# Linear attention by pairs of heads, V projected with tokens on the partitions, C_acc in the memory of X

## The reference

```python
q, k, v = silu(xn @ w_qkv)              # xn: layer norm of x; per head 128 wide
g = sigmoid(xn @ w_gate)
for each block of tokens:               # the kernel takes blocks of 128
    inter = (q * q_decay) @ kv
    intra = ((q @ k.T) * diag_decay) @ v
    kv = block_decay * kv + (k * k_decay).T @ v
    o = inter + intra
x = x + (rms_norm(o over all heads) * rms_weight * g) @ w_out
```

## Time and profile before

| | |
|---|---|
| median of 3 runs | 3095.34 us (3094.22 to 3097.39) |
| the profiled execution | 3093.59 us |
| its span, first to last instruction | 3091.8 us |
| TensorE, VectorE, ScalarE, GpSimd busy | 2803.0, 1804.6, 1466.3, 793.4 us |
| granted TensorE clock, mean of the span | 0.932 |
| DMA | 193.65 MB, mean 63 GB/s |
| L1789, projections of the linear attention | 342.6 + 322.6 + 321.3 us busy in 3 x 1032 matmuls |
| L1813, transposes VT | 77.2 us busy in 516 |
| L1749, ScalarE's copy of VT | 76.4 us busy in 129 |

### The profile page before, as it was taken

One profiled execution on the slowest core, in us unless ns is written; L12 is line 12 of the kernel. 1 busy time (PEld: TensorE's weight loads), 2 busy tenths in 40 slices (PEclk: granted clock), 3 DMA queues, 4 the chain that ended last, 5 costly groups with the idle time before them and its releaser, 6 DMA issues. The chain is left out here.

```text
span 3091.8 us, 51426 instructions
## 1 busy us (share of the span) xinstructions
PE 2803.0 (91%) x17564; PEld 2237.6 (72%) x17564; DVE 1804.6 (58%) x3284; ACT 1466.3 (47%) x2689; POOL 793.4 (26%) x812
## 2 busy tenths in 40 slices
PE   5689999979889999599999999999999999978573
PEld 4534444448668888488888888988888898868452
DVE  5378888826678887555555555555555545556421
ACT  5337777766468877433333333333333333334110
POOL 2412212210052222022222222222222222214675
PEclk9879999999989999699999999999999999975575
DMA  4875655230064543000000000000000000002376
GB/s 145 238 102 75 84 69 74 30 94 3 4 224 186 189 177 136 23 11 0 10 10 10 10 10 3 8 10 10 10 10 10 0 10 10 8 27 88 90 173 123
DMA packets 159113, 193.65 MB, mean 63 GB/s; under 512 B 18257, under 2 KB 135537, under 8 KB 150257
## 3 DMA queue, kind: packets, MB, share of 16 engines
q1 hardware_dynamic: 150464, 177.10, 21.9%
q0 software_dynamic: 8544, 15.22, 2.9%
HBM read 149.89 MB, written 46.58 MB: 64 GB/s over the span
## 5 line engine op out<-in xcount | busy, mean ns | idle before, releaser
L744 DVE TENSOR_REDUCE score_pm<-score_SM 128x1 f32<-128x512 f32 (+3 forms) x608 | 364.2, 655 | 124.1 <-PE score_SM L613 73.3
L1718 POOL TENSOR_TENSOR lin_o2sum<-lin_o2sum,lin_o 128x512 f32<-128x512 f32 x128 | 165.8, 1296 | 1049.2 <-ACT lin_o L1754 1049.2
L1933 DVE SCALAR_TENSOR_TENSOR lin_go<-lin_gT,lin_O 128x512 f32<-128x512 f32 x128 | 88.0, 688 | 477.0 <-ACT lin_o L1754 477.0
L704 ACT ACTIVATE score_PR<-score_SE 128x512 f32<-128x512 f32 (+1 forms) x640 | 309.9, 557 | 106.0 <-PE score_SE L638 102.6
L1789 PE MATMUL lin_PJ<-C_XH,lin_WH 128*128 128x512 f32 x1032 | 342.6, 413 | 13.1 <-DVE lin_WL L1893 13.1
L1789 PE MATMUL lin_PJ<-C_XL,lin_WH 128*128 128x512 f32 x1032 | 322.6, 394 | 0.0
L1789 PE MATMUL lin_PJ<-C_XH,lin_WL 128*128 128x512 f32 x1032 | 321.3, 393 | 0.0
L1950 DVE TENSOR_TENSOR C_acc<-lin_OUT,C_acc 128x512 f32<-128x512 f32 x256 | 177.0, 692 | 142.0 <-PE lin_OUT L1824 139.6
L610 PE MATMUL score_SM<-score_KR,score_QR 96*128 96x512 bf16 (+3 forms) x768 | 230.2, 341 | 28.2 <-DMA score_V<-v_rows 25.5
L1737 ACT ACTIVATE lin_qT<-lin_PJ 128x512 f32<-128x512 f32 x129 | 76.9, 596 | 376.2 <-PE lin_PJ L1789 376.2
L1789 PEld LDWEIGHTS lin_PJ<-C_XH,lin_WL 128*128 128x128 f32 x1032 | 194.3, 188 | 44.9
(11 more groups left out here) (351 smaller groups left out, 6398.7 us busy)
## 6 DMA issues: line engine op xcount, KB each, us to landing
experts_sq<-B_roots SPq DMA_DIRECT2D x64, 1024.0 KB, 4.7
score_QR<-q_parts SPq DMA_DIRECT2D x96, 128.0 KB, 7.1
score_KR<-k_parts SPq DMA_DIRECT2D x96, 128.0 KB, 7.7
kept_GU<-L_ffn_gate_up_proj SPq DMA_DIRECT2D x48, 192.0 KB, 3.1
v_rows<-qkv_vt SPq DMA_DIRECT2D x32, 256.0 KB, 2.6
score_V<-v_rows SPq DMA_DIRECT2D x16, 512.0 KB, 10.8
C_w<-L_attn_w_qkv SPq DMA_DIRECT2D x51, 128.0 KB, 2.3
q_parts<-qkv_parts SPq DMA_DIRECT2D x16, 384.0 KB, 2.6
```

The costliest lines, as they stand in the source:

```text
L704: nc.scalar.activation(PR[:, st % BUFS, h, 0:width], SE[:, e % RING, 0:width], ACT.Exp, scale=SCALE)\
L744: nc.vector.tensor_reduce(pm[:, n % 2, h0:h0 + nh, t, k0 // CHUNK], SM[:, count % RING, 0:nh * nk].rearrange("p (h k) -> p h k", h=nh), AX ...
L1718: nc.gpsimd.tensor_tensor(o2sum[:, c], o2sum[:, c], o2[:], ALU.add).then_inc(pool_sum, 1)
```

## The change

Three edits that belong together.

1. The loop runs over 8 pairs of heads, 16 turns each: for every chunk c, head j = 0, then j = 1. Weights, decays and output weights are loaded, split and scaled for two heads at once (tiles twice as large), once a pair. Each head of the pair has its state kv[:, j].
2. V is projected with tokens on the partitions, for both heads at once: the stationary operand is the tile of tokens, the moving one the 256 columns of the two heads' weights. One call makes two of the four sequences (12 matmuls of 256 columns into the bank VP), so the two turns of a chunk make v for the next chunk of both heads. Silu reads VP and writes v; the tile vT, the transposes VT and the copy are gone. G uses the bank that V had used with Q.
3. C_acc lies in the memory of X. X is stored to DRAM (`x_rows`, 4 MB) in lnC's prefetches; its first 8 tiles are loaded into x_first during the linear attention, the other 24 at the start of the ranking, in three loads that SP issues ahead of its stores and that `variances` waits for.

```diff
@@ transpose_phase prefetch, linear_attention_layer
+                  (x_rows.rearrange("(t p) n -> p t n", p=P), X[:]),
                   (gate[:], a["L1_ffn_gate_weight"].rearrange("(k p) n -> p k n", p=P)),
@@ linear_attention_phase
-        vT = ph.sb("vT", [P, B4, BLK])
-        v = ph.sb("v", [P, B4, DH])
+        v = ph.sb("v", [P, 2, B4, 2 * DH])
-        kv = ph.sb("kv", [P, B4, DH])
+        kv = ph.sb("kv", [P, 2, B4, DH])
-        VT = ph.ps("VT", [P, B4, P])
+        VP = ph.ps("VP", [P, 2, 2 * DH])
+        HP, TURNS = H // 2, 2 * NBLK
+        LAST = NBLK - 1
@@ ScalarE
-            def vg(n, u):
-                act.wait_ge(pe_v, done(n))
-                nc.scalar.activation(vT[:], PJ[:, 0], ACT.Silu).then_inc(act_v, 1)
+            def values(m, slot, half):
+                act.wait_ge(pe_v, done(m))
+                nc.scalar.activation(v[:, slot, 2 * half:2 * half + 2, :], VP[:], ACT.Silu).then_inc(act_v, 1)
+
+            def gates(n, u):
                 act.wait_ge(dve_go, done(n - 2))
                 act.wait_ge(pe_g, done(n))
-                nc.scalar.activation(gT[:, u], PJ[:, 1], ACT.Tanh, scale=0.5).then_inc(act_g, 1)
-                act.wait_ge(pe_vt, done(n))
-                nc.scalar.activation(v[:], VT[:], ACT.Copy).then_inc(act_vt, 1)
+                nc.scalar.activation(gT[:, u], PJ[:, 0], ACT.Tanh, scale=0.5).then_inc(act_g, 1)
...
+                    if (c, j) != (LAST, 1):
+                        qk(i + 1, 1 - j)
                         square(i)
                         gated_high(i)
+                        if c < LAST:
+                            values(g * TURNS + 2 * (c + 1) + j, (c + 1) % 2, j)
+                        gates(i + 1, 1 - j)
                     else:
+                        weights_high(g + 1)
                         square(i)
                         gated_high(i)
+                        qk(i + 1, 0)
+                        values(i + 1, 0, 0)
+                        gates(i + 1, 0)
+                        values(i + 2, 0, 1)
@@ TensorE
+            def project_g(n, c, j):
+                pe.wait_ge(act_q, done(n))
+                project(0, G, c, j, pe_g)
+
+            def project_v(m, c, half, load):
                 if c == 0:
                     pe.wait_ge(wl_ready, 2 * load + 2)
+                pe.wait_ge(act_v, done(m - 1))
+                for b in range(2):
+                    n = 0
+                    for x, a in ((xh, WH), (xl, WH), (xh, WL)):
+                        for k in range(KD):
+                            ins = nc.tensor.matmul(VP[:, b, :], x[:, k, 2 * half + b, c, :], a[:, V, k, :],
+                                                   start=(n == 0), stop=(n == 3 * KD - 1))
+                            n += 1
+                ins.then_inc(pe_v, 1)
...
+            project_qk(0, 0, 0, 0)
+            project_v(0, 0, 0, 0)
+            project_g(0, 0, 0)
+            project_v(1, 0, 1, 0)
...
+                    if (c, j) != (LAST, 1):
+                        project_qk(i + 1, c + j, 1 - j, g)
+
+                    pe.wait_ge(act_v, done(g * TURNS + 2 * c + 1))
                     pe.wait_ge(dve_sd, done(i))
                     pe.wait_ge(pool_qd, done(i))
                     pe.wait_ge(dve_go, done(i - 1))
...
                     pe.wait_ge(dve_kd, done(i))
+                    if c < LAST:
...
                         ins.then_inc(pe_kv, 1)
-                        project_vg(i + 1, c + 1, h)
-                        output(i, h)
+                        project_v(g * TURNS + 2 * (c + 1) + j, c + 1, j, g)
+                    if (c, j) != (LAST, 1):
+                        project_g(i + 1, c + j, 1 - j)
+                        output(i, g, j)
                     else:
-                        project_qk(i + 1, 0, h + 1)
-                        output(i, h)
-                        project_vg(i + 1, 0, h + 1)
+                        project_qk(i + 1, 0, 0, g + 1)
+                        project_v(i + 1, 0, 0, g + 1)
+                        output(i, g, j)
+                        project_g(i + 1, 0, 0)
+                        project_v(i + 2, 0, 1, g + 1)
@@ ranking_phase
         def _(sp):
+            for r in range(1, RUNS):
+                sp.dma_start(x_of(r * RT, RT), x_rows[r * RT * P:(r + 1) * RT * P, :].rearrange("(t p) n -> p t n", p=P))\
+                    .then_inc(x_in[r - 1], 16)
...
             def variances(run):
                 tiles = range(run * RT, (run + 1) * RT)
+                if run:
+                    dve.wait_ge(x_in[run - 1], 16)
@@ build_program
+        x_at = nc.sbuf_base - TILES * D * 4
-        acc = keep("C_acc", [P, TILES, D])
+        acc = nc.alloc_sbuf_tensor_at("C_acc", [P, TILES, D], F32, offset=x_at)
```

More of the change, by code:

```diff
@@ L11 @@
+import itertools
 from contextlib import ExitStack
@@ L1704, in _ @@
             give_credit(pool, pool_qd, pool_sum)
-            with pool.Fori(0, H) as h:
-                for c in range(NBLK):
-                    i, u = h * NBLK + c, c % 2
+            with pool.Fori(0, HP) as g:
+                for c, j in itertools.product(range(NBLK), range(2)):
+                    i = g * TURNS + 2 * c + j
                     pool.wait_ge(act_q, done(i))
@@ L1722, in _ @@
             act.preload_act_table(ACT.Silu)
-            give_credit(act, act_q, act_k, act_v, act_g, act_vt, act_sq, act_goh)
+            give_credit(act, act_q, act_k, act_v, act_g, act_sq, act_goh)
             def weights_high(load):
                 act.wait_ge(w_in, (load + 1) * 64)
-                act.wait_ge(pe_g, done(load * NBLK - 1))
-                for pair in PAIRS:
+                act.wait_ge(pe_g, done(load * TURNS - 1))
+                act.wait_ge(pe_v, done(load * TURNS - 1))
+                for pair in PARTS:
                     nc.scalar.activation(WH[:, pair], raw[:, pair], ACT.Copy).then_inc(wh_ready, 1)
@@ L1823, in output @@
                         for n, (x, w) in enumerate(((goh, WOH), (goh, WOL), (gol, WOH))):
-                            ins = nc.tensor.matmul(OUT[:, half, b, :], x[:, 2 * half + b, :], w[:],
+                            ins = nc.tensor.matmul(OUT[:, half, b, :], x[:, 2 * half + b, :], w[:, j],
                                                    start=(n == 0), stop=(n == 2))
                     ins.then_inc(pe_out[half], 1)
[L1828 to L1832, removed]
+            project_qk(0, 0, 0, 0)
+            project_v(0, 0, 0, 0)
+            project_g(0, 0, 0)
+            project_v(1, 0, 1, 0)
+            with pe.Fori(0, HP) as g:
+                for c, j in itertools.product(range(NBLK), range(2)):
+                    i = g * TURNS + 2 * c + j
                     pe.wait_ge(act_k, done(i))
@@ L1904, in _ @@
             weights_low(0, 0)
             weights_low(0, 1)
-            weights_out(0, rms[:, 0:1])
-            with dve.Fori(0, H) as h:
-                for c in range(NBLK):
-                    i, u = h * NBLK + c, c % 2
-                    if c == 0:
+            weights_out(0, (slice(0, 1), slice(1, 2)))
+            with dve.Fori(0, HP) as g:
+                for c, j in itertools.product(range(NBLK), range(2)):
+                    i, h = g * TURNS + 2 * c + j, g * 2 + j
+                    if (c, j) == (0, 0):
@@ L1958, in _, with linear_attention_layer @@
             nc.vector.reciprocal(rs[:], rs[:])
-def linear_attention_layer(nc, a, X, ident, decays, kdec, bdec, acc, rs, gate, o2n):
+def linear_attention_layer(nc, a, X, ident, decays, kdec, bdec, acc, rs, gate, o2n, x_rows, x_first):
     with ExitStack() as c:
@@ L1982, with ranking_phase @@
 JOINS = 4
-def ranking_phase(nc, raw, o2n, X, acc, rs, ident, rows, out, idx):
-    RUNS = 4
-    RT, RC = TILES // RUNS, CHUNKS // RUNS
+def ranking_phase(nc, raw, o2n, x_rows, x_first, acc, rs, ident, rows, out, idx):
     HI, LO = CAP // 8, 8
@@ L2075, in now, with x_of @@
             return i - back if 0 <= i - back < CHUNKS else None
+        x_in = [ph.sem(f"x_in{r}") for r in range(1, RUNS)]
+        def x_of(t, n=1):
+            return x_first[:, t:t + n, :] if t < RT else x_rest[:, t - RT:t - RT + n, :]
         def tiles_of(g):
@@ L2614, in _, with capacity_moe_layer @@
                     indices((e + S - 2) % KEPT, (u + S - 2) % S)
-def capacity_moe_layer(nc, a, X, ident, out, odd, rows, acc, rs, raw, o2n):
+def capacity_moe_layer(nc, a, x_rows, x_first, ident, out, odd, rows, acc, rs, raw, o2n):
     with ExitStack() as c:
         idx = c.enter_context(nc.sbuf_tensor("D_idx", [CAP, KEPT], U32))
-        ranking_phase(nc, raw, o2n, X, acc, rs, ident, rows, out, idx)
+        ranking_phase(nc, raw, o2n, x_rows, x_first, acc, rs, ident, rows, out, idx)
         kept_experts_phase(nc, a, rows, out, odd, idx, ident)
@@ L2640, in build_program @@
         o2n = keep("D_o2n", [P, 1], I32)
-        acc = keep("C_acc", [P, TILES, D])
+        acc = nc.alloc_sbuf_tensor_at("C_acc", [P, TILES, D], F32, offset=x_at)
         rs = keep("C_rs", [P, TILES])
```

(6 more changed lines are left out.)

225 lines of the change are left out of this document (110 added, 115 removed).

## The result

The changed kernel takes 3121.33 us (median of 4 runs, 3119.63 to 3121.63); the kernel before, measured beside it on the same chip, 3096.36 (4 runs, 3094.22 to 3098.32). The ratio is 1.0077, with a 95% interval of 1.0064 to 1.0089: slower by 25.0 us, or 0.8%. The profiled execution has a span of 3119.5 us at a mean granted clock of 0.926, against 3091.8 at 0.932.

A forecast was written before the change was run, and what follows sets the result against it. TensorE, tied with the chain square, o2sum, qd, gol, was taken to bound the loop. Turns +4.8 and stage start and end +1.0 gave +5.8 on the median: 3101.1 us; likeliest range 3094 to 3105, overall 3092 to 3121 (about 0.84).

The forecast's parts named there:

- a tie: Linear-attention loop: TensorE's own path and the chain through gol end within 0.01 us, so TensorE could not start the output earlier.
- the 54 us of removed work on TensorE: V projection and transposes: TensorE's work falls 0.42 us a turn, 54 us over 128 turns, a reading the prediction rejected.
- normal turns: Most turns of the loop: stay 11.42 us, gain 0.00, at most 0.05, because the output waits for gol.
- Rival A: Whole loop: TensorE's own path decides, so the saving shows, -50 us to 3045; chance 0.14.
- (7,0): Turn of chunk 7, head 0 of a pair: 11.42 us, with some 2.7 us of idle TensorE.
- (0,1): Turn of chunk 0, head 1 of a pair: 8 fewer O matmuls, 10.68 us.
- (0,0): Turn of chunk 0, head 0 of a pair: the transposes fall away, 13.85 - 0.42 = 13.43 us.
- no cost for X: X's store to DRAM and loads back: taken as 0, with bounds of +1.5 us (store) and +2 us (loads).
- rival B: Idle 2.7 us in (7,0) drops the clock to 1.2 GHz, costing 2.0 us, 8 times 16: 3117; chance 0.09.
- The start: Start of the linear-attention stage: doubled WL step +0.56 us, two V projections instead of one +1.40, less VT's 0.45.
- the end: End of the linear-attention stage, behind the last output: VT and the copy fall away, -0.5 us.
- The bounds of the sum: Limits around the whole sum of +5.8 us: 112 x 0.05 = 5.6 us less and 3.5 more.

The follow-up runs named there:

- runs 1 and 2: One added wait, GpSimd's o2sum only after gol: in the changed kernel 3055.29 us (ratio 0.986), in the kernel before 3094.98 us (ratio 0.9988).
- run 1: Changed kernel with one added wait, so GpSimd begins o2sum and the next qd only when gol is done: 3055.29 us, ratio 0.986.
- run 8: Kernel before with only X's store to DRAM, its later loads and C_acc in X's memory, heads one by one: 3097.27 us, ratio 1.0004.
- run 4: Changed kernel with the four compute engines' loops over the pairs written out whole, no jump back: 3104.86 us, ratio 1.0023.
- run 3: Kernel before with two heads written out in each pass of four engines' loops, work and order unchanged: 3121.39 us, ratio 1.0077.
- run 6: Changed kernel with Q and K of the pair's last turn projected behind O of the turn before it: 3099.0 us, ratio 1.0011.
- run 5: Changed kernel with 12 extra, unused matmuls of 256 columns between G and the output in turn (7,0): 3113.44 us, ratio 1.0059.

## Why the prediction was right or wrong

**Right: the bound.** That busy 198.5 of 200 hid a tie between TensorE's own path and the chain square, o2sum, qd, gol is what runs 1 and 2 show, and that the 54 us of removed work on TensorE would not show in normal turns holds to 0.01 us a turn. Rival A (3045, the gain is real) fell for the change as it stands. It came true where qd was put behind gol: run 1's 0.43 a normal turn against its 0.42.

**Right: (7,0), (0,1), X, and (0,0) without the jump.** 11.38 for 11.42, 10.68 for 10.68, no cost for X (run 8), and 13.36 in run 4 for 13.43.

**Wrong: a term was missing.** The sum for (0,0) counted what the turn's work costs, and took from the earlier trace rows that a jump costs what it did before. The body's length doubled; I counted that nowhere. Here it is 1.3 to 1.6 over the forecast at each jump, seven times, about 10 us; run 4 takes 18 of the 25 us away (the jumps, 0.17 in each (0,1) and some of the clock falls), and run 3 brings 23 to the kernel before with no other change.

**Wrong: rival B had too small a chance.** I gave the clock's fall 0.09 with the argument that idle stretches of 0.53 had left the clock at 1.00. That row says nothing of 2.7 us, five times as long; between 0.53 (no fall) and 13.55 (at 1.2 GHz behind it) I had no row, so 2.7 was open and wanted a chance near one half. Its price was also too high: 2.0 in all eight pairs, where it was 1.5 in six. The 2.0 took the projections of the earlier trace rows as what runs slowly; in fact it was the output's last matmuls, the S product and the KT transposes, 3.4 us long.

**Small terms.** The start cost 1.14, not 1.5, and the end gave 1.8, not 0.5: the two together +1.0 forecast, -0.7 measured, beside a stage that began 0.79 later. The bounds of the sum give 3095.5 as the lower end of the likeliest's own range, not the 3094 that stands there.

**The whole.** 3101.1 was forecast, 3121.3 came: past the range's upper end of 3121.0 by 0.3 us, and inside it, at 3119.2, if the measured ratio is put on the median shown before. Rival B's time (3117) is nearer, but for a part of the wrong reason: the clock brought 9 us, the jumps 10. The side was right, the likeliest value 20 us low. That the time lies at the range's edge and not far outside is luck: the range reached so far because B was priced too high, and half of what filled it was a cost that stands nowhere in the prediction.

**What is open.** Why TensorE stands about 3.2 us behind a jump in run 3 and 0.95 to 1.48 in the changed kernel; what the engines do in that time, since the profile names only "issue" (that it is the fetching of code is my reading of the packets on q8, and no run shows it apart from the body's length); why the clock didn't fall in two of eight equal places, nor at six of run 3's seven jumps. Run 6 is +3.5 us though its way from first to last output is 1.1 shorter than before (1435.15 against 1436.25): its first output comes 2.9 later (1.6 of it is an lnC that ends later, 1.3 the longer start), and from its last output to the end it takes 1.7 more. But for the 1.3 these parts have no cause shown, and they are no larger than what the profiles of like kernels differ by there.

## What to carry to other kernels

An engine that is busy 99% of the time can still be in a tie with a chain through three others: before costing a removed step, read what ends at the same moment as it, and remove both. Here one wait that orders GpSimd behind VectorE's short step is worth 66 us in the changed kernel (9 of them by the clock) and 3 in the kernel before, and in the normal turns the removed transposes are worth nothing without it. When a change doubles the body of a hardware loop, look in the list of waits for "issue" at the first instructions behind the jump; and when it opens an idle stretch on TensorE as long as the 2.4 us here, move independent matmuls there.

## What was new about the hardware

- **A jump back in a long body.** Behind it VectorE stood 2.98 to 3.22 us and TensorE 0.95 to 1.48 in the changed kernel, 2.71 to 3.04 and 2.96 to 3.38 in run 3; in the kernel before, whose body is half as long, it was 0.25 at most on VectorE and nothing on TensorE, and nothing to speak of in run 4 without a jump (0.05 at most). The packets on q8 were 57 before, 146 and 145 with the long body, 130 in straight code.
- **The granted clock behind short idle stretches.** Behind 2.42 us of idle TensorE the clock was at 1.2 GHz for 3.4 us in 6 of 8 cases (4 of 8 in run 4), and each fall cost 1.2 to 1.6 us; behind 1.0 (run 5) or 1.5 (run 1, 11.7 us on PE in 8) it never fell in this loop. Length alone does not decide: behind the 2.7 to 3.2 us at run 3's jumps it fell in 1 of 7.
- **One GpSimd operation between two VectorE operations.** The same gol took 1.68 behind qd and 0.69 ahead of it, in all 128 turns of run 1.
